# More filler matmuls, no norm steps for the padding pair, the second feed-forward product copied out one step earlier, its bias added by GpSimd

## What is computed

```
x = x + conv_experts(ln_c(x))                     # router picks 1 of 4 experts: 3x3 depthwise, gelu, 1x1
t = t + ffn0(ln_t(t))                             # per pixel, 48 -> 192 -> 48
x = x + mamba_dct(ln_c(x))                        # DCT, norm, 4 quadrants, selective scan, inverse DCT
t = t + ffn1(ln_t(t))

def ffn(x):                                       # q_mul: e5m2, q_acc: e5m10 (fp16)
    h = relu(q_acc(q_acc(q_mul(x) @ q_mul(W1).T) + q_mul(b1)))
    return q_acc(q_acc(q_mul(h) @ q_mul(W2).T) + q_mul(b2))
```

## Time and profile before

| | |
|---|---|
| time, three runs | 4181.06 us median (4176.02 to 4199.72) |
| the profiled execution | 4180.93 us, of which the span in the profile is 4179.1 |
| PE, DVE, ACT, POOL busy | 3691.1, 3529.6, 2770.7, 2348.2 us |
| granted TensorE clock, mean | 0.965 |

### The profile page before, as it was taken

One profiled execution on the slowest core, in us unless ns is written; L12 is line 12 of the kernel. 1 busy time (PEld: TensorE's weight loads), 2 busy tenths in 40 slices (PEclk: granted clock), 3 DMA queues, 4 the chain that ended last, 5 costly groups with the idle time before them and its releaser, 6 DMA issues.

```text
span 4179.1 us, 41686 instructions
## 1 busy us (share of the span) xinstructions
PE 3691.1 (88%) x13960; PEld 1340.0 (32%) x13960; DVE 3529.6 (84%) x3149; ACT 2770.7 (66%) x3212; POOL 2348.2 (56%) x1092
## 2 busy tenths in 40 slices
PE   7799988999889998899988998889998899878887
PEld 2422234222442224422243223432234222342223
DVE  5689976999769997699967998779987799768997
ACT  2667656776567766677566775667757677576764
POOL 1168741787318773277722876238752578426873
PEclk9899999999999999999999999999999999998888
DMA  1288842898338882488725887258861798508881
GB/s 41 58 205 207 211 109 63 210 223 202 88 84 221 214 198 63 125 214 205 173 78 142 202 220 169 63 142 215 213 163 47 175 217 212 133 20 198 199 206 43
DMA packets 186381, 644.72 MB, mean 154 GB/s; under 512 B 25708, under 2 KB 26648, under 8 KB 182712
## 3 DMA queue, kind: packets, MB, share of 16 engines
q1 hardware_dynamic: 169144, 596.95, 59.0%
q10 hardware_dynamic: 17024, 45.10, 3.6%
HBM read 525.40 MB, written 78.82 MB: 145 GB/s over the span
## 4 chain that ended last, share of the span: by engine, by line
DVE 36%; issue 24%; PE 18%; ACT 13%; DMA 5%; POOL 3%; DVEq 0%; ACTq 0%; POOLq 0%; SPq 0%
DVE ps L1611 14%; DVE arena L1616 13%; DMA arena<-dl 4%; PE ps L684 4%; PE ps L624 3%; PE ps L675 2%; ACT arena L1056 2%; ACT arena L1038 2%; POOL arena L1727 2%; ACT arena L1263 2%; POOL arena L1718 2%; DVE arena L1429 2%; PE ps L856 1%; PE ps L879 1%; ACT arena L1049 1%
## 5 line engine op out<-in xcount | busy, mean ns | idle before, releaser
L1718 POOL TENSOR_TENSOR arena<-arena 128x1024 f32<-128x1024 f32 x760 | 1785.4, 2359 | 703.4 <-DVE arena L1616 703.4
L1616 DVE TENSOR_TENSOR_SCAN arena<-arena,ps 128x1024 f32<-128x1024 f32 x768 | 1756.3, 2287 | 74.4 <-issue 31.6
L1263 ACT ACTIVATE arena<-arena,a_all 128x1024 f32<-128x1024 f32 x768 | 868.4, 1144 | 708.0 <-DMA arena<-dl 566.6
L856 PE MATMUL ps<-arena,spread 32*128 32x512 f32 x1536 | 877.1, 652 | 140.3 <-DVE arena L1616 138.3
L1611 DVE TENSOR_TENSOR ps<-ps,arena 128x1024 f32<-128x1024 f32 x768 | 929.0, 1210 | 64.3 <-PE ps L858 64.1
L858 PE MATMUL ps<-arena,spread 32*128 32x512 f32 x1536 | 870.2, 653 | 0.0
L879 PE MATMUL ps<-arena,gather 128*32 128x512 f32 x3072 | 523.2, 633 | 11.7 <-DVE arena L1627 11.7
L950 PE MATMUL ps<-x 96*96 96x512 f32 x1008 | 500.3, 614 | 25.1 <-ACT arena L1194 25.1
L856 PEld LDWEIGHTS ps<-arena,spread 32*128 32x128 f32 x1536 | 230.1, 186 | 786.3 <-DVE arena L1616 470.4
L1676 POOL TENSOR_TENSOR x<-x,arena 96x512 f32<-96x512 f32 x64 | 113.9, 1779 | 377.3 <-DVE arena L1420 377.3
L1015 ACT ACT_TABLE_LOAD x226 | 290.0, 1283 | 7.4 <-DMA eps<-in_eps 3.4
(11 more groups left out here) (165 smaller groups left out, 4865.9 us busy)
## 6 DMA issues: line engine op xcount, KB each, us to landing
arena<-dl SPq DMA_DIRECT2D x880, 512.0 KB, 6.9
dl<-arena ACTq DMA_DIRECT2D x64, 384.0 KB, 5.8
x<-pn SPq DMA_DIRECT2D x56, 247.5 KB, 10.7
arena<-in_x SPq DMA_DIRECT2D x8, 1536.0 KB, 13.0
arena<-xq SPq DMA_DIRECT2D x64, 192.0 KB, 6.3
arena<-arena ACTq DMA_DIRECT2D x64, 192.0 KB, 7.5
out<-x SPq DMA_DIRECT2D x64, 192.0 KB, 2.1
arena<-xq SPq DMA_DIRECT2D x64, 191.8 KB, 5.6
```

The costliest lines, as they stand in the source:

```text
L856: pe.matmul(ps[:, bank, :], spread[rows[0], r, :], u[rows[0], i, 0:512], start=True, stop=True)
L1263: act.activation(da[:, m % DAS, :], dbc[:, m % DBC, :], ACT.Exp, scale=a_all[:, v // 2, m:m + 1]).then_inc(da_ready, 1)
L1616: dve.tensor_tensor_scan(hs[:, m % HSS, :], da[:, m % DAS, :], driven, 0.0, ALU.mult, ALU.add).then_inc(h_ready, 1)
L1718: pool.tensor_tensor(product, product, cmat[:, v % 2, :], ALU.mult).then_inc(pr_ready, 1)
```

## The change

- **Fillers.** 18 in place of 16 at the start, and 3 more (same kind) in each step of the first norm stream. `keep_warm` gets a bank as argument and is also called at three places of each turn: 2 calls before the wait for the norms and the router, 3 after the router, 5 before the normed turn.
- **No padding norm steps.** Pair 6's stream has 16 parts in place of 24; `stream_steps` keeps it running until the next pair's `turn_in` is done. Its load of the padding x, the wait for it and the zeroing of borders go too.
- **Copy out one step sooner.** DVE copies the second product in step j + 3, behind the norm product (and the sum) of that step.
- **The bias** `yb` is computed by POOL, just ahead of the addition that it already did, in place of DVE.

```diff
-WARM_EARLY = 16
+WARM_EARLY, WARM_STEP = 18, 3
+WARM_CENTRE, WARM_MASK, WARM_NORM = 2, 3, 5
...
+        def ln_count(p):
+            return p * LN_PAIR + LN_FIRST - (NCH if p == PAIRS - 1 else 0)
...
-        def stream_parts(first, last):
-            if first:
+        def stream_parts(p):
+            if p < 0:
                 return ("ffn0",) * NCH + ("norm",) * NCH
-            if last:
+            if p == PAIRS - 1:
                 return ("ffn1",) * NCH
+            if p == PAIRS - 2:
+                return ("ffn1",) * NCH + ("ffn0",) * NCH
             return ("ffn1",) * NCH + ("ffn0",) * NCH + ("norm",) * NCH
 
+        def stream_steps(parts):
+            ffns = sum(part != "norm" for part in parts)
+            return max(len(parts) + 3, ffns + 3 + NG if "ffn0" in parts else 0)
+
         def turned_in(parts, t):
-            n = t - len(parts) + 6
+            n = t - sum(part != "norm" for part in parts) - 2
...
                     sync.dma_start(x[:], a["xsp"]).then_inc(x_back, 16)
-                    sync.wait_ge(mo_copied, (p + 1) * 2 * QUADS)
-                    sync.dma_start(xin, a["x"][p + 2]).then_inc(x_in, 16)
+                    if p + 2 < PAIRS:
+                        sync.wait_ge(mo_copied, (p + 1) * 2 * QUADS)
+                        sync.dma_start(xin, a["x"][p + 2]).then_inc(x_in, 16)
...
                     if 0 <= t - 1 < len(parts):
                         j, n = (t - 1) % NCH, n0 + t - 1
+                        if parts[0] == "norm":
+                            warm_early(WARM_STEP)
                         pe.wait_ge(squared, n + 1)
...
+                keep_warm(WARM_CENTRE)
+                pe.wait_ge(normed, ln_count(p))
                 if not last:
                     router(p + 2)
+                keep_warm(WARM_MASK)
...
+                keep_warm(WARM_NORM, 7)
                 turn(lambda g: pix[:, g, :], 128, R, by_half(D_NORMED2))
...
-                for t in range(1, len(parts) + 4):
-                    if is_ffn(parts, t - 4):
-                        j = t - 4
-                        dve.wait_ge(fc2_ready, f0 + j + 1)
-                        if j >= 2:
-                            dve.wait_ge(yb_ready, f0 + j - 1)
-                        dve.tensor_copy(yf[:, j % 2, :], ps[0:R, 7, :]).then_inc(yf_ready, 1)
+                for t in range(1, stream_steps(parts) + 1):
                     if is_ffn(parts, t - 1):
...
+                    if is_ffn(parts, t - 3):
+                        j = t - 3
+                        dve.wait_ge(fc2_ready, f0 + j + 1)
+                        if j >= 2:
+                            dve.wait_ge(yb_ready, f0 + j - 1)
+                        dve.tensor_copy(yf[:, j % 2, :], ps[0:R, 7, :]).then_inc(yf_ready, 1)
                     if is_ffn(parts, t - 2):
...
-                    if is_ffn(parts, t - 4):
-                        j = t - 4
-                        layer = int(parts[j] == "ffn1")
-                        dve.wait_ge(yf_ready, f0 + j + 1)
-                        if j >= 2:
-                            dve.wait_ge(ffn_done, f0 + j - 1)
-                        dve.tensor_scalar(yb[:, j % 2, :], yf[:, j % 2, :], b2[:, layer:layer + 1], None,
-                                          ALU.add).then_inc(yb_ready, 1)
...
             def ffn(layer, f0, stored):
                 for j in range(NCH):
+                    pool.wait_ge(yf_ready, f0 + j + 1)
+                    pool.tensor_scalar(yb[:, j % 2, :], yf[:, j % 2, :], b2[:, layer:layer + 1], None,
+                                       ALU.add).then_inc(yb_ready, 1)
                     pool.wait_ge(yb_ready, f0 + j + 1)
```

More of the change, by code:

```diff
@@ L578, in _, with warm_early @@
             pe.wait_ge(early_in, EARLY_IN)
-            for _ in range(WARM_EARLY):
-                pe.matmul(ps[R:128, 7, 0:R], average[:, 0:128 - R], average[:], start=True, stop=True)
+            def warm_early(count):
+                for _ in range(count):
+                    pe.matmul(ps[R:128, 7, 0:R], average[:, 0:128 - R], average[:], start=True, stop=True)
+            warm_early(WARM_EARLY)
             def take_middle(P):
@@ L616, in stream @@
             def stream(n0, f0, parts, ready, src, P):
-                for t in range(len(parts) + 3):
+                for t in range(stream_steps(parts)):
                     if 0 <= t - 1 < len(parts):
                         j, n = (t - 1) % NCH, n0 + t - 1
+                        if parts[0] == "norm":
+                            warm_early(WARM_STEP)
                         pe.wait_ge(squared, n + 1)
@@ L724, in _, with keep_warm @@
                               start=True, stop=True).then_inc(pw_ps, 1)
-            stream(NCH, 0, stream_parts(True, False), first_ready, {"ffn0": col, "norm": xin}, 0)
+            stream(NCH, 0, stream_parts(-1), first_ready, {"ffn0": col, "norm": xin}, 0)
+            def keep_warm(count, bank=0):
+                for _ in range(count):
+                    pe.matmul(ps[DI:128, bank, :], gather[:, 0, :], spread[:].rearrange("p r m -> p (r m)"),
+                              start=True, stop=True, skip_group_check=True)
             def pair(p, last):
-                pe.wait_ge(normed, p * LN_PAIR + LN_FIRST)
+                keep_warm(WARM_CENTRE)
+                pe.wait_ge(normed, ln_count(p))
                 if not last:
                     router(p + 2)
+                keep_warm(WARM_MASK)
                 def by_half(step):
@@ L782, in of_xi @@
                                      start=True, stop=True)
-                def keep_warm(count):
-                    for _ in range(count):
-                        pe.matmul(ps[DI:128, 0, :], gather[:, 0, :], spread[:].rearrange("p r m -> p (r m)"),
-                                  start=True, stop=True, skip_group_check=True)
                 def prep_first():
@@ L1003, in ready @@
                         pe.wait_ge(x_in, (p + 3) * 16)
-                stream(p * LN_PAIR + LN_FIRST, p * 2 * NCH + NCH, stream_parts(False, last), ready,
+                stream(ln_count(p), p * 2 * NCH + NCH, stream_parts(p), ready,
                        {"ffn1": x, "ffn0": col, "norm": xin}, p + 1)
@@ L1102, in _ @@
             act.wait_ge(setup_dve, 1)
-            stream(NCH, 0, stream_parts(True, False), 0)
+            stream(NCH, 0, stream_parts(-1), 0)
             def roots(p):
@@ L1330, in rest @@
                 evac(p, T_BACK, flat(pix), 128, GB * R)
-                stream(p * LN_PAIR + LN_FIRST, p * 2 * NCH + NCH, stream_parts(False, last), p + 1)
+                stream(ln_count(p), p * 2 * NCH + NCH, stream_parts(p), p + 1)
             roots(0)
@@ L1517, in _ @@
                 conv_taps(t)
-            stream(NCH, 0, stream_parts(True, False), 2, 0)
+            stream(NCH, 0, stream_parts(-1), 2, 0)
             assert steps[0] == PROLOGUE, steps
@@ L1529, in both_norms @@
             def both_norms(p, last):
-                base[0], steps[0] = p * CHAIN + PROLOGUE, 0
+                base[0], steps[0] = p * CHAIN + PROLOGUE - (p == PAIRS - 1), 0
                 a0 = p * LN_ACT
@@ L1649, in rest @@
                     dve.tensor_tensor(part, part, ps[0:R, c, :], ALU.add).then_inc(pix_dve, 1)
-                stream(p * LN_PAIR + LN_FIRST, p * 2 * NCH + NCH, stream_parts(False, last), 2 * (p + 2), p + 1)
-                assert last or steps[0] == CHAIN, steps
+                stream(ln_count(p), p * 2 * NCH + NCH, stream_parts(p), 2 * (p + 2), p + 1)
+                assert last or steps[0] == CHAIN - (p == PAIRS - 2), steps
             linked = both_norms(0, False)
@@ L1745, in pair @@
                 scan_stage(prep, lambda: None, step, conv, final)
-                if not last:
+                if p + 2 < PAIRS:
                     pool.wait_ge(mo_copied, (p + 1) * 2 * QUADS)
```

4 lines of the change are left out of this document (2 added, 2 removed).

## The result

Changed kernel: median 4156.7 us of 18 executions (4140.2 to 4205.0), kernel before: 4179.9 of 18 (4162.2 to 4199.7). Ratio 0.9948, 95% interval 0.9931 to 0.9965: 0.5% faster, where I had forecast 4100 us and 2%. Ratios leave out executions that are more than 1.5% above the fastest of their kernel: one here (4205.0) and three in the last of these sessions. The profiled execution is the fastest of the 18, 4140.2 us, so the two profiles differ by 40.7 us where the medians differ by 23.

What follows compares the result with a forecast made beforehand. No engine alone bounds the kernel, but a chain of waits, priced stage by stage. Savings 36.3 + 24 + 9.5 + 11.5 = 81.3 us from 4180.9 give 4099.6, say 4100 us; range 4084 to 4138.

Steps and rivals of the forecast that it cites:

- Copy-out and bias: Feed-forward steps: early copy-out and bias on POOL cut a step from 3.745 to 3.40 us, 36.3 us together.
- POOL as the cover: Feed-forward steps: POOL's bias takes 0.85 us, so POOL needs 2.75 to 3.15 a step, under 3.40, and keeps up.
- POOL becomes the bound: Rival, feed-forward steps: bias takes 1.4 us or more, the 36.3 gone from about 1.45; time 4136 to 4142; chance 0.13.
- DVE still fits: Feed-forward steps: DVE's copy-out, waiting for the second product, is done just before the next relu is due.
- Turn fillers: Turns of all 8 pairs: fillers end before DVE is ready and hold PE's clock, 3.0 us a pair, 24 us.
- Opening: First norm stream: three fillers a step raise the clock, steps go from 4.40 to 3.02 us, 9.5 us saved.
- Padding norm: Pair 6's stream: without norm steps on padding the turn-in shrinks from 18.2 to about 7.5 us; 11.5 saved, once.
- alone, a turn is PE-bound at about 0.9: Pair 6's turn-in without norm work: each turn takes about 0.9 us, so eight take 7.2.
- The chance of 0.04 for slower: Rival, whole kernel slower: POOL's bias at 1.85 us or more, step 4.15; a bias of 2.2 gives 4220; chance 0.04.
- faster and level, 0.91 and 0.05: Whole kernel: chance 0.91 of faster by more than about 0.5% (21 us), 0.05 of within 0.5%.
- half of 0.06, 0.04 and 0.04: Chances left out of faster: last half of turn fillers not holding the clock (4124 to 4150), slower, and nothing that shows.

Runs made afterwards that it cites:

- the last of these sessions: The changed kernel, unaltered, run again beside the kernel before: median 4220.1 us of eight, ratio 1.0069.
- experiments 1: Changed kernel with the bias back on VectorE, behind the cast; copy-out still one step early: 4113.0 us, ratio 0.9833, step 3.45 us.
- 3: Changed kernel with the copy-out back at its old place, at the head of the step after, bias still on POOL: 4266.9 us, one execution, step 4.31.
- 6: Changed kernel with POOL's addition cut to 8 of 512 columns, its bias whole: 4205.5 us, one execution, steps 3.87 or 4.33 us.
- tail_warm: Changed kernel with 2, 3 and 5 more filler matmuls in the last three steps of pair 6's stream: 4140.9 us, one execution; that stream 79.6 for 84.2.

## Why the prediction was wrong

- **Copy-out and bias (-36.3, measured about +2).** The step that failed is "POOL as the cover": "I take 0.85, the middle", bounds 0.52 to 1.15. The bias takes 1.56 with nothing of VectorE beside it (pair 6's last, at 3663 us of the changed kernel) and 2.38 in its place. The rival "POOL becomes the bound" had the threshold (1.45) and the time (4136 to 4142; the profile was 4140) but not the mechanism, so the fit to this profile is luck. I charged the contention to POOL alone (0.65 for a cast, from the earlier trace rows); it goes both ways, and VectorE's part, 0.28 us on the cast, stands on a loop that my sum waved through with "DVE still fits": cast, product, copy-out, relus, cast. Without the bias on POOL that loop is 3.45, near my 3.40; even then the eight other streams give 25.0 us (620.1 to 595.1) of my 31.6. Shown by experiments 1, 3 and 6.
- **What the move could win.** My sum did see that the bias between relu and cast costs little (0.08; measured 0.05). So the risk was taken for nothing, and the sum should have said so: the early copy-out alone brought 3.745 to 3.48.
- **Turn fillers (-24).** Right: -24.5 in the profile, 26.5 when taken out alone. The granted clock is 1.00 through all eight turns of the profile.
- **Opening (-9.5, profile -11.7).** About the right number, by luck: the profile happened to have a fast opening. Openings are fast or slow from one execution to another, with and without fillers. What decides is open: the kernel before was slow twice, and the same 16 fillers in two other kernels were fast.
- **Padding norm (-11.5, measured -2.9 to -4.9).** The step "alone, a turn is PE-bound at about 0.9" took a row at full clock. Without norm work PE waits 1.39, 2.12 and 3.05 us for the last casts and does the turns at 1.2 GHz. The work removed had kept the clock up: with fillers in its place (tail_warm) it stays at 1.00.
- **Not in the sum at all: scatter.** The sum is of one execution. The bias on POOL lengthens PE's wait at each stream's end from 1.17 to 1.31, 1.56 or 2.01 us, and after the longest a stream mostly goes on at 1.2 GHz, at up to 14.4 us each. In the first session this cost little, in two others it turned the change into a loss. The chance of 0.04 for slower was too low. The chances for faster and level, 0.91 and 0.05, also do not add up as described: leaving out half of 0.06, 0.04 and 0.04 gives 0.89 and 0.07.

## What to carry to other kernels

An elementwise operation moved from VectorE to GpSimd must be priced twice: its own time beside VectorE's fp16 work, and what it adds to that work; who comes first has a say in who pays, and here the shift of one copy-out changed the price on VectorE fourfold. An operation that fills a gap between two dependent ones can be nearly free where it stands (0.34 us long, it cost 0.05 here): look at the distance of the starts, not at its duration. Taking work from TensorE, or lengthening one of its waits, can cost the clock of the stage behind; time such a change in more than one session.

## What was not expected of the hardware

- GpSimd's 96x512 fp16 tensor_scalar took 1.56 us, more than its two-input fp32 addition of the same size (1.15).
- Beside it VectorE's 128x1536 cast took 0.95, 1.23 or 1.41 us, and 1.77 beside the addition.
- In slow openings the granted clock is given as 1.00 while the same average takes 2.02 us for 1.10. The column is no reading there: these traces hold no record of the clock before 61 to 65 us (the fast ones from 7 to 10 us on), and where there is none it says 1.00. At the start of the span the durations tell the clock.
- How POOL's bias meets VectorE in one step (second relu 0.34 or 0.78 us, cast 0.96, 1.15 or 1.41) decides a wait of PE of 1.31, 1.56 or 2.01 us. On 14 of the 15 longest a fall of the clock followed, on 1 of the other 42.
